# A small rank-16 product on TensorE: from f32 operands to packed fp32r high and low parts

## The reference, cut to what matters

```python
y = jnp.einsum('bsd,od->bso', x, weight) + bias
seg = jnp.searchsorted(lora_start_indices, jnp.arange(B), side='right') - 1
adapter_idx = jnp.clip(seg - 1, 0, lora_A.shape[0] - 1)
A = lora_A[adapter_idx]        # 3 adapters of rank 16, A: 16 x 1024, B: 1024 x 16
Bw = lora_B[adapter_idx]
lo = jnp.einsum('bsr,bor->bso', jnp.einsum('bsd,brd->bsr', x, A), Bw)
return y + jnp.where((seg > 0)[:, None, None], lo, 0)
...
x = x + 0.5 * ffn(layernorm(x))
x = x + attention(layernorm(x))
x = x + 0.5 * ffn(layernorm(x))
```

## Time and profile before

| | us |
|---|---|
| median of 3 runs | 1931.37 |
| lowest, highest | 1930.92, 1934.0 |
| profiled execution | 1932.19 |
| its span, first to last instruction | 1930.3 |
| PE busy | 1807.9 (94%) |
| DVE busy | 1231.7 (64%) |
| first linear layer, pieces 0 to 15 made | 12.65 to 138.8 |

### The profile page before, as it was taken

The page is one execution under the profiler, slowest core; times in us unless marked ns, Lnnn a source line. Parts: engine busy times, 40 slices in busy tenths (PEclk is TensorE's granted clock), DMA queues, the critical chain, the costliest instruction groups (busy, mean ns, idle before and its releaser), DMA issues. The chain is left out here.

```text
span 1930.3 us, 44295 instructions
## 1 busy us (share of the span) xinstructions
PE 1807.9 (94%) x15472; PEld 1419.5 (74%) x15472; DVE 1231.7 (64%) x2653; ACT 999.0 (52%) x2135; POOL 871.8 (45%) x641
## 2 busy tenths in 40 slices
PE   6999959899999999999999999995799999968999
PEld 3678859777777777777777777773688888857887
DVE  5555348789888898888988888885421211125453
ACT  2211047788788887888878888783411100012210
POOL 2232112377787877878778787782000000014321
PEclk9999979999999999999999999998899999989999
DMA  6542153321222212222122221211742332225321
GB/s 225 173 159 103 55 166 97 83 64 41 84 68 67 77 41 84 68 67 71 46 84 67 67 68 50 84 63 62 256 131 87 103 115 87 66 109 175 120 88 65
DMA packets 111697, 182.48 MB, mean 95 GB/s; under 512 B 27472, under 2 KB 64464, under 8 KB 109584
## 3 DMA queue, kind: packets, MB, share of 16 engines
q1 hardware_dynamic: 111632, 181.61, 29.1%
HBM read 122.06 MB, written 59.51 MB: 94 GB/s over the span
## 5 line engine op out<-in xcount | busy, mean ns | idle before, releaser
L1040 PE MATMUL psS<-keyT,q 128*128 128x512 f32 (+2 forms) x2304 | 472.2, 350 | 24.5 <-POOL q L568 14.9
L1040 PEld LDWEIGHTS psS<-keyT,q 128*128 128x128 f32 x2304 | 380.5, 189 | 118.5 <-DVE negmax L1146 41.8
L1105 ACT ACTIVATE prob<-prob,negmax 128x640 f32<-128x640 f32 (+7 forms) x512 | 392.4, 769 | 77.7 <-DVE negmax L1146 75.0
L1156 DVE STREAM_TRANSPOSE pT<-prob 128x640 f32<-128x640 f32 (+7 forms) x512 | 380.0, 762 | 66.3 <-PE psV L1057 61.7
L1146 DVE CUSTOM_DVE_ANT_0 prob<-psS,mask 128x640 f32<-128x640 f32 (+7 forms) x512 | 371.8, 742 | 20.2 <-PE psS L1040 7.3
L419 PE MATMUL f_psy<-f_weff,f_xT 128*128 128x512 f32 x1344 | 313.8, 393 | 0.0
L1368 PE MATMUL o_psy<-o_w,o_o 128*128 128x512 f32 x1344 | 304.8, 389 | 0.0
L1368 PEld LDWEIGHTS o_psy<-o_w,o_o 128*128 128x128 f32 x1344 | 252.3, 188 | 52.3
L419 PEld LDWEIGHTS f_psy<-f_weff,f_xT 128*128 128x128 f32 x1344 | 250.9, 188 | 53.9 <-issue 1.7
L1057 PE MATMUL psV<-pT,val 32*64 32x512 f32 (+3 forms) x8192 | 265.8, 408 | 6.7 <-DVE pT L1156 6.2
L1057 PEld LDWEIGHTS psV<-pT,val 32*64 32x64 f32 x8192 | 169.1, 132 | 110.8 <-issue 67.2
(11 more groups left out here) (113 smaller groups left out, 1911.1 us busy)
## 6 DMA issues: line engine op xcount, KB each, us to landing
wo<-in_wo SPq DMA_DIRECT2D x16, 1024.0 KB, 6.0
pT<-row_scales SPq DMA_DIRECT2D x128, 128.0 KB, 2.8
oT<-pT SPq DMA_DIRECT2D x64, 256.0 KB, 2.5
o_in<-oT SPq DMA_DIRECT2D x32, 512.0 KB, 5.3
f_xt<-in_x SPq DMA_DIRECT2D x16, 512.0 KB, 4.3
f_w_in<-in_w SPq DMA_DIRECT2D x16, 512.0 KB, 6.6
w_sum<-f_w_in SPq DMA_DIRECT2D x16, 512.0 KB, 5.2
x<-f_xo SPq DMA_DIRECT2D x16, 512.0 KB, 2.9
```

Source lines behind the costliest of these rows:

```text
L1040: ins = nc.tensor.matmul(psS[:, slot, start + x0:start + x1], q[:, e, a, t * P:(t + 1) * P], k.keyT[:, m, b * S + x0:b * S + x1], start=(i ...
L1105: nc.scalar.activation(row, row, ACT.Exp, bias=negmax[:, n % 8:n % 8 + 1], scale=-1.0, accum_out=rowsum[:, column(n, s):column(n, s) + 1]) ...
L1156: nc.vector.transpose(pT[:, n % 2, t, 0:width], prob[:, n % RING, 0:width]).then_inc(turned, 1)
```

## The change

Rows of A and B are packed, 48 rows and 16 of zeros, and laid twice into 128 partitions. B is split into a high part `b_hi` (both halves) and a low part `b_lo` (upper rows B minus its high part, lower rows zero). `gated` is fp32r: A's high part in partitions 0 to 63, A's low part (A minus its high part, made in place) in 64 to 127. So gated x `b_hi` gives high x high and low x high in one product of 128 rows, and gated x `b_lo` gives high x low. Each bank gets two fp32r products in place of one f32 product. A and B lie in the two halves of `f_xo`, and POOL's `add_bias` waits until both entries are gated. `wanted` is loaded instead of set.

```diff
-            lora_a = c.sb("lora_a", [GATED, D])
-            lora_b = c.sb("lora_b", [GATED, D])
-            gated = c.sb("gated", [GATED, B, D])
+            lora_a, lora_b = xo[:, 0, :], xo[:, 1, :]
+            b_lo = c.sb("lora_b_lo", [P, D], F32R)
+            b_hi = c.sb("lora_b_hi", [P, D], F32R)
+            gated = c.sb("gated", [P, B, D], F32R)
...
-                a_d, b_d, starts_d = adapters
-                sp.dma_start(starts[:], starts_d.rearrange("(a n) -> a n", a=1).to_broadcast([GATED, STARTS])).then_inc(starts_in, 16)
-                sp.dma_start(lora_a[:], a_d[:, :]).then_inc(a_in, 16)
-                sp.dma_start(lora_b[:], b_d[:, :]).then_inc(b_in, 16)
+                a_d, b_d, starts_d, wanted_d = adapters
+                sp.dma_start(starts[:], starts_d.rearrange("(a n) -> a n", a=1).to_broadcast([P, STARTS])).then_inc(starts_in, 16)
+                sp.dma_start(wanted[:], wanted_d[:, :]).then_inc(starts_in, 16)
+                for rows in (slice(0, PACKED), slice(PACKED, P)):
+                    sp.dma_start(lora_b[rows, :], b_d[:, :]).then_inc(b_in, 16)
+                for rows in (slice(0, PACKED), slice(PACKED, P)):
+                    sp.dma_start(lora_a[rows, :], a_d[:, :]).then_inc(a_in, 16)
...
+                elif w_d is not None:
+                    pool.wait_ge(gate, B)
                 nc.gpsimd.tensor_tensor(xo[:, j, :], f.xt[:, j, :], bias_half[:], ALU.add).then_inc(with_bias, 1)
...
-                for a in range(ADAPTERS):
-                    nc.gpsimd.memset(wanted[32 * a:32 * a + 32, :], float(a + 2)).then_inc(numbered, 1)
+                nc.gpsimd.memset(f.xn[PACKED:P, 1, :], 0.0).then_inc(cleared, 1)
+                pool.wait_ge(cleared, 1)
+                nc.gpsimd.tensor_copy(b_lo[PACKED:P, :], f.xn[PACKED:P, 1, :]).then_inc(b_rest, 1)
+                pool.wait_ge(b_split, 1)
+                nc.gpsimd.tensor_tensor(b_lo[0:PACKED, :], lora_b[0:PACKED, :], b_hi[0:PACKED, :].bitcast(F32),
+                                        ALU.subtract).then_inc(b_rest, 1)
...
+            if w_d is not None:
+                act.wait_ge(b_in, 32)
+                nc.scalar.activation(b_hi[:], lora_b, ACT.Copy).then_inc(b_split, 1)
+                act.wait_ge(a_in, 32)
+                nc.scalar.activation(gated[:, 0, :], lora_a, ACT.Copy).then_inc(a_split, 1)
             pieces_hi([0])
...
-                    ins = nc.tensor.matmul(ps_w[:, half, :], gated[:, i // DT, (i % DT) * P:(i % DT + 1) * P],
-                                           lora_b[:, half * BANK:(half + 1) * BANK], start=True, stop=True)
+                    x, y = slice((i % DT) * P, (i % DT + 1) * P), slice(half * BANK, (half + 1) * BANK)
+                    nc.tensor.matmul(ps_w[:, half, :], gated[:, i // DT, x], b_hi[:, y], start=True, stop=False)
+                    ins = nc.tensor.matmul(ps_w[:, half, :], gated[:, i // DT, x], b_lo[:, y], start=False, stop=True)
...
+            def adapters_lo():
+                dve.wait_ge(a_split, 1)
+                nc.vector.tensor_tensor(lora_a[PACKED:P, :], lora_a[PACKED:P, :],
+                                        gated[PACKED:P, 0, :].bitcast(F32), ALU.subtract).then_inc(a_rest, 1)
+                dve.wait_ge(a_rest, 1)
```

More of the change, by code:

```diff
@@ L33 @@
 STARTS = 4
-GATED = 32 * ADAPTERS
+PACKED = 64
 QT = S // P
@@ L220, in ffn_phase @@
             ps_w = c.ps(tag + "ps_w", [P, 2, BANK])
-            lora_a = c.sb("lora_a", [GATED, D])
-            lora_b = c.sb("lora_b", [GATED, D])
-            gated = c.sb("gated", [GATED, B, D])
[L224 to L229, removed]
+            lora_a, lora_b = xo[:, 0, :], xo[:, 1, :]
+            b_lo = c.sb("lora_b_lo", [P, D], F32R)
+            b_hi = c.sb("lora_b_hi", [P, D], F32R)
+            gated = c.sb("gated", [P, B, D], F32R)
+            starts = c.sb("starts", [P, STARTS], I32)
+            startf = c.sb("startf", [P, STARTS])
+            hit = c.sb("hit", [P, B, STARTS])
+            count = c.sb("count", [P, B])
+            wanted = c.sb("wanted", [P, 1])
+            chosen = c.sb("chosen", [P, B])
             starts_in, a_in, b_in = c.sem("starts_in"), c.sem("lora_a_in"), c.sem("lora_b_in")
-            numbered, chain, gate = c.sem("numbered"), c.sem("chain"), c.sem("gate")
+            chain, gate, cleared = c.sem("chain"), c.sem("gate"), c.sem("lora_cleared")
+            a_split, b_split, a_rest, b_rest = c.sem("lora_a_hi"), c.sem("lora_b_hi"), c.sem("lora_a_lo"), c.sem("lora_b_lo")
         bias_in, halved = c.sem(tag + "bias_in"), c.sem(tag + "halved")
@@ L326, in _ @@
             if w_d is not None:
-                for a in range(ADAPTERS):
-                    nc.gpsimd.memset(wanted[32 * a:32 * a + 32, :], float(a + 2)).then_inc(numbered, 1)
+                nc.gpsimd.memset(f.xn[PACKED:P, 1, :], 0.0).then_inc(cleared, 1)
[4 more added lines that the diff above has]
+                                        ALU.subtract).then_inc(b_rest, 1)
+                pool.wait_ge(b_rest, 2)
             pieces_low([0])
@@ L375, in outer_products @@
                 else:
-                    pe.wait_ge(b_in, 16)
+                    pe.wait_ge(b_split, 1)
+                    pe.wait_ge(b_rest, 2)
                 if i % DT == 0:
@@ L443, in link @@
                     dve.wait_ge(chain, next(links))
-                dve.wait_ge(starts_in, 16)
-                dve.wait_ge(numbered, ADAPTERS)
+                dve.wait_ge(starts_in, 32)
                 link(nc.vector.tensor_copy(startf[:], starts[:]))
@@ L451, in choose @@
                     link(nc.vector.tensor_scalar(chosen[:, b:b + 1], count[:, b:b + 1], wanted[:, 0:1], None, ALU.is_equal))
+            def adapters_lo():
[3 more added lines that the diff above has]
+                dve.wait_ge(a_rest, 1)
             def gate_of(b):
-                dve.wait_ge(a_in, 16)
-                nc.vector.tensor_scalar(gated[:, b, :], lora_a[:], chosen[:, b:b + 1], None, ALU.mult).then_inc(gate, 1)
+                nc.vector.tensor_scalar(gated[:, b, :], lora_a, chosen[:, b:b + 1], None, ALU.mult).then_inc(gate, 1)
             def results(n, j):
@@ L469, in _ @@
             if w_d is not None:
+                adapters_lo()
                 gate_of(0)
@@ L1376, in output_steps, with macaron_block @@
     steady(eng, step, NT, 1, 1, start=0)
-def macaron_block(nc, x, wa, lnw, wn, wpe, wv, wo, cos, sin, cosT, sinT, w, bias, lora_a, lora_b, starts, out):
+def macaron_block(nc, x, wa, lnw, wn, wpe, wv, wo, cos, sin, cosT, sinT, w, bias, lora_a, lora_b, starts, wanted, out):
     x1_d = nc.dram_tensor("x1", (T, D), F32).ap()
@@ L1395, in macaron_block @@
         constants_phase(nc, k)
-        ffn_phase(nc, "f1_", k, x, x1_d, bias, sum_d, w, (lora_a, lora_b, starts))
+        ffn_phase(nc, "f1_", k, x, x1_d, bias, sum_d, w, (lora_a, lora_b, starts, wanted))
         with ExitStack() as inner:
@@ L1448 @@
     blank = _np.zeros((NOPE, S), _np.float32)
-    blank_rows = _np.zeros((ADAPTERS, 32 - RANK, D), _np.float32)
+    blank_rows = _np.zeros((PACKED - ADAPTERS * RANK, D), _np.float32)
+    wanted = _np.concatenate([_np.repeat(_np.arange(2.0, ADAPTERS + 2.0), RANK), _np.zeros(PACKED - ADAPTERS * RANK)])
     data = {
@@ L1466 @@
         "bias": get("L0_ffn_bias"),
-        "lora_a": _np.concatenate([get("L0_ffn_lora_A"), blank_rows], 1).reshape(GATED, D),
-        "lora_b": _np.concatenate([get("L0_ffn_lora_B").transpose(0, 2, 1), blank_rows], 1).reshape(GATED, D),
+        "lora_a": _np.concatenate([get("L0_ffn_lora_A").reshape(ADAPTERS * RANK, D), blank_rows], 0),
+        "lora_b": _np.concatenate([get("L0_ffn_lora_B").transpose(0, 2, 1).reshape(ADAPTERS * RANK, D), blank_rows], 0),
         "starts": get("L0_ffn_lora_start_indices"),
+        "wanted": _np.concatenate([wanted, wanted]).astype(_np.float32).reshape(P, 1),
     }
```

## The result

| | before | changed |
|---|---|---|
| median | 1933.04 us (1930.65 to 1937.14) | 1928.95 us (1925.9 to 1929.48) |
| ratio | 1 | 0.9975, 95% interval 0.9967 to 0.9983 |
| profiled execution | 1932.19, span 1930.3 | 1928.94, span 1926.9 |

The changed kernel is faster by 4.8 us (interval 3.3 to 6.4), where 4.5 were forecast. The forecast time was 1926.9 us, and 1928.95 were measured: the kernel before has a median of 1933.04 over these 12 executions, 1.7 us above the 1931.37 of three that the forecast started from. The profiled execution came out at 1928.94 where the sum gave 1927.7.

What follows compares the result with a forecast made beforehand. PE, busy 94% of the span, was taken as the bound except in head, ramp and passage into the steps. Gains of 0.3 + 1.0 + 3.2 = 4.5 us from the median 1931.37 gave 1926.9 us, range 1924.5 to 1929.3.

Steps and rivals of the forecast that it cites:

- Products: PE's outer products: four fp32r products of 0.229 us replace two f32 ones, 0.92 us against 1.72, saving 0.80 each where PE-bound.
- Head: Before sum(0): new loads, roundings, subtractions and gate have no cover, so sum(0) starts at 17.7, 1.4 us late.
- A is eaten ahead of the steps: Rival: a costlier head puts sum(0) at 18.5 or 20, cutting the gain to 3.7 to 2.2 us; chance 0.28.
- Ramp: From sum(0) to tile 2's turn: 1.4 us lateness travels on, then PE bounds; turn at 60.5 against 60.86, 0.3 us gained.
- Passage: Outer products 9 to 11, before tile 5's turn: 0.80 us each would bring PE there 2.7 us sooner, at 91.6.
- rival D: PE's clock stays low after less work and a longer pause; slower by over 0.2%, about 1938 us; chance 0.05.
- The wait at tile 5: Turn at 94.27 waits for normalised tile 5 and comes at 93.0; gain there 1.3 us, 1.4 of PE's saving lost.
- The sum: Whole kernel: 0.3 from the ramp, 1.0 at tile 5's turn and 3.2 from outer products 12 to 15 give 4.5 us.

Runs made afterwards that it cites:

- head_alone: Changed kernel's new head (loads, roundings, subtractions, gates) with f32 tiles and one f32 product a bank as before the change; 1936.9 us, ratio 1.0021.
- low_b_on_dve: Changed kernel with the subtraction for B's low part moved from POOL to DVE, ahead of that for A; 1929.56 us, ratio 0.998.
- changed_again: The changed kernel run once more with nothing edited; 1930.08 us, ratio 0.9979.
- a_first: Changed kernel with A loaded and rounded ahead of B; 1929.58 us, ratio 0.9978.
- bias_first: Changed kernel with POOL adding the next tile's bias ahead of its low parts in the first layer's steps; 1928.51 us, ratio 0.9972.
- best: bias_first with A loaded ahead of B, B's low part by DVE behind the gate, and PE's products with B's high part first; 1926.84 us, ratio 0.9963.
- high_only_bias_first: high_only with POOL adding the next tile's bias ahead of its low parts in the first layer's steps; 1924.72 us, ratio 0.995.
- ramp_bias_first: Changed kernel with POOL adding the bias to tile 1 before the low part of piece 2, ahead of the first step; 1928.31 us, ratio 0.9974.
- high_only: Changed kernel without the product of gated and B's low part, two fp32r products a piece instead of four; 1927.95 us, ratio 0.9972.

## Why the prediction was right, step by step

- **Products.** 0.23 us each in the steps, and 12.72 us a step (12.7 forecast): right. The last four gave 3.08 us, for 3.2.
- **Head.** Root ended at 10.26 (10.3), A landed at 11.5 (11.6), gate ended at 15.51 (15.7), PE at 15.66 (15.7), sum(0) at 17.82 (17.7): right. The low part of A met POOL in one execution (2.12 us) and hardly in the other (1.33), so that term is not a fixed 1.0. The row it was read from was a good one: DVE's instruction ended 1.08 us after POOL's there, and 1.09 here both times.
- **A is eaten ahead of the steps** (0.28): the mechanism is real, as head_alone shows with 2.4 us, but its price was the one in the sum.
- **Ramp.** Statistics of tile 3 at 42.98 (43.2), sum(6) at 48.92 (49.2), turn of tile 2 at 60.40 (60.5): right in number. The reason given was too simple. "Everything to there is 1.4 us late" holds for a later head (head_alone: 2.66 in, 2.23 out); an earlier one is absorbed by the load's longer transfer (low_b_on_dve: 0.87 in, 0.04 out). In the changed kernel itself sum(0) was 1.54 late; then the slow turn of tile 1 added 0.5, which the prediction did not have: POOL's first `add_bias` started at 31.05 for 28.98, and the load was issued 2.16 late. From sum(0) to this issue went 19.65 us in head_alone, 19.87 before, and 20.49 to 20.51 in changed, changed_again, low_b_on_dve, a_first, bias_first and best, in the order of that turn's 1.10, 1.45 and 1.97 us. So the issue follows the head whole, earlier or later, and what is absorbed is absorbed in the transfer. The load took 4.6 us instead of 5.7, so the statistics were 1.13 late where 1.4 was forecast. Two terms were left out, of opposite sign, some 0.6 and 1.0 us; that the number came out is partly luck.
- **Passage.** Here a term was mis-sized. "With 0.80 each" for outer products 9 to 11 should have brought PE to the turn of tile 5 2.7 us sooner; it was ready at 93.04 - 0.55 = 92.49, 1.78 sooner. Outer product 9 ran at the low clock and gave nothing (1.87 us to the next turn, 1.82 before), and the turn behind it took 1.79 us instead of 1.04. That is what rival D described, and the low pace up to 26.7 us (below) is the other place of it; in the changed kernel it did not spread further.
- **The wait at tile 5.** Right in place and cause (bias_first, high_only_bias_first); 0.55 us and not 1.4, since PE came 0.9 later. The two errors cancel, since the turn waits for the tile and not for PE: it is at 93.04 for 93.0.
- **The sum.** 148.24 - 143.93 = 4.3 of the forecast 4.5 us at the end of the pieces. The span shows 3.4. Of the 0.9 between them, 0.2 lie in the steps without a piece, which last 11.81 us each in the changed kernel and 11.77 before; why is open. The rest of the kernel, from the next layer's first turn to the end, lasted between 1674.8 and 1677.5 us in all twelve profiles of this case (before 1675.4, changed 1676.1, changed_again 1676.4). That is a wide spread for single executions, and 0.7 is well inside it, but the two kernels with f32 outer products are among the lowest three, so a small cost there is not excluded. The ratio, over more executions, says 4.8.

**Open.** Why PE was slow at 23.7 and at 64.2 us. At the first place the wait is not what began it. In the changed kernel products stood 0.43 us apart from the first ones on (from 19.69 to 20.12, for instance) and came to 0.23 only at 26.7. Before, outer product 1 at 17.56 took 1.98 us, as much as outer product 9 at the full clock, and the granted clock was 0.50 from 23 to 26 us. At the second place the granted clock was 0.82 from 60 to 69.5 us in every kernel with fp32r outer products, and 1.00 in both with f32 ones, before and head_alone, whose wait was 2.77 us as well; head_alone has the new head, too. So neither that wait nor the head is enough for it. Nor does the slow stretch begin with the wait's end in every kernel: in bias_first and ramp_bias_first outer product 9 still starts its products 0.23 us apart, and the turn behind it takes 1.68 and 1.91 us. There is a third place, in some kernels only: from 40 to 45 us the granted clock was 0.66 to 0.69 in high_only, high_only_bias_first, low_b_on_dve, a_first and bias_first, and 1.00 in the other seven. Whether it is the kind of product or how PE is loaded ahead of the wait no run here separates.

## What to carry to other kernels

A saving on the busiest engine counts only from the last place where that engine waits for something else: halving these products once more gave nothing until another engine's order was changed. Ask of each edit in a prologue what releases the next load, because a later start is passed on while an earlier one may only lengthen a transfer. And price new preparatory work by a run of its own: here the new head cost 2.4 us, over a third of the 6.7 us between head_alone and the changed kernel.

## What the runs showed of the hardware beyond this

- DVE's subtraction of two SBUF inputs (64 x 1024) took 1.22 us alone and 1.33 to 2.12 beside a GpSimd one, ending 1.08 to 1.09 us after it; the low part of piece 3 (128 x 1024) took 3.51 us where it met two of GpSimd's in a row, and 1.23 alone. Both ways: GpSimd's 2.4 us became 3.44 in high_only.
- The four transfers of 256 KB into 64 partitions landed some 1.2 us apart (7.9, 9.2, 10.3, 11.5), 218 GB/s, where 384 KB into 96 partitions had 269 in the earlier trace rows. The Trainium skill (SBUF — State Buffer, "Door 1: The DMA port swizzle") gives transfers into partitions 0 to 63 a rate of 196 GB/s at 1 MiB and about 218 GB/s as the limit. The trace's 218 agrees with the limit, at 256 KB already, and not with the 269 of my sum. The Trainium skill (SBUF — State Buffer, "Can I just issue two DMAs to hit both halves?") also says that two transfers into the two halves go one after the other. The trace agrees: they landed 1.2 us apart. A still landed at 11.5 and not at the 13.1 estimated from 196 GB/s, as the first half of B landed at 7.9, sooner than both estimates had it.
- A granted clock of 1.00 in the record was no proof of a fast PE in the first 25 us: in the changed kernel it read 1.00 from 22 to 26 us, while the eight transposes at 23.70 took 1.97 us, against 1.04 for the same eight at 60.40.
